# A two-layer decoder on one core: the order of projections, expert batches and rotations in layer 0, and six places in place of four in layer 1

## The reference

```python
# layer 0
qkv = x @ w_qkv.T                        # 32 query heads, 8 key/value heads, 64 wide
q, k = rope(rms(q) * wq), rope(rms(k) * wk)
a = softmax(q @ k.T / 8 + window_mask) @ v       # group "a"
x = layernorm(x + a @ w_out.T)           # norm x1; projection "out0"
q, k, v = x @ Wq, x @ Wk, x @ Wv         # 32 heads, 8 wide, rope
a  = softmax(q @ k.T + mask) @ v                 # "x", head groups 0..7, masked
a += tanh(gate) * softmax(q @ ak.T) @ av         # "x", groups 8..15, the adapter: keys and values of ctx
x = layernorm(x + a @ Wo)                # norm x2; projection "outx"
cw = top6(softmax(x @ gate_w.T))
for e in range(16):                      # experts, 176 wide
    y += cw[:, e] * (silu(x @ wg[e].T) * (x @ wu[e].T)) @ wd[e].T
x = layernorm(x + y)                     # norm x3
# layer 1: causal attention (16 heads), then attention of every row over all 1,024 rows of ctx
p = round(255 * softmax(q @ k.T)) / 255          # 16 heads x 8 tiles
x = layernorm(x + (p @ v) @ Wp + bp)
# then a gated feed-forward block with fp8-rounded weights
```

## Time and profile before

| | |
|---|---|
| median of 3 runs | 1586.13 us (1580.53 to 1587.86) |
| the profiled execution | 1585.61 us, of it 1583.70 us from the first to the last instruction |
| PE busy | 1339.4 us, 85% |
| DVE busy | 1078.7 us, 68% |
| ACT busy | 692.6 us, 44% |
| POOL busy | 112.0 us, 7% |
| granted TensorE clock, mean | 0.888 |
| layer 0 | to about 1107 us |
| causal attention of layer 1 | about 1107 to 1264 us |
| heads loop | about 1264 to 1480 us |
| feed-forward block | to the end |

### The profile page before, as it was taken

One profiled execution on the slowest core, in us unless ns is written; L12 is line 12 of the kernel. 1 busy time (PEld: TensorE's weight loads), 2 busy tenths in 40 slices (PEclk: granted clock), 3 DMA queues, 4 the chain that ended last, 5 costly groups with the idle time before them and its releaser, 6 DMA issues.

```text
span 1583.7 us, 24579 instructions
## 1 busy us (share of the span) xinstructions
PE 1339.4 (85%) x9229; PEld 881.4 (56%) x9234; DVE 1078.7 (68%) x2477; ACT 692.6 (44%) x1286; POOL 112.0 (7%) x95
## 2 busy tenths in 40 slices
PE   3868998998998999899899899999899678887576
PEld 1635765765765676576576567656777422222334
DVE  4458567556846756755684675564788789888577
ACT  1325434523632543452363254252444288787332
POOL 2020011002002001100200200000000000000001
PEclk9989999999999999999999999999999755555589
DMA  8200100100100010010010003100200089899300
GB/s 335 89 11 13 57 7 14 56 10 14 56 11 4 13 57 7 14 56 11 14 56 11 1 13 119 56 16 9 90 8 8 1 154 162 160 170 152 55 1 28
DMA packets 174517, 83.97 MB, mean 53 GB/s; under 512 B 137920, under 2 KB 170048, under 8 KB 173888
## 3 DMA queue, kind: packets, MB, share of 16 engines
q1 hardware_dynamic: 173248, 82.03, 21.1%
q10 hardware_dynamic: 1152, 0.36, 0.1%
HBM read 43.57 MB, written 5.24 MB: 31 GB/s over the span
## 4 chain that ended last, share of the span: by engine, by line
PE 47%; DVE 28%; issue 6%; ACT 6%; DMA 5%; POOL 1%; DVEq 0%; POOLq 0%; ACTq 0%
PE ps_p L1602 11%; PE ps_t L1618 10%; PE ps_s L1799 6%; DMA w_moe<-w_moe 5%; DVE w_moe L1491 4%; PE ps_o L1836 3%; DVE probs L1084 3%; PE ps_o L1679 3%; DVE row_max L1090 2%; PE ps_o L1799 2%; PE ps_p L1656 2%; PE ps_o L1683 2%; PE ps_t L1627 2%; PE ps_s L1656 1%; DVE probs L1075 1%
## 5 line engine op out<-in xcount | busy, mean ns | idle before, releaser
L1618 PE MATMUL ps_t<-ident,probs 128*128 128x128 f32 x1072 | 176.0, 286 | 27.6 <-ACT probs L820 11.3
L820 ACT ACTIVATE probs<-probs 128x512 f32<-128x512 f32 x192 | 120.9, 630 | 150.1 <-DVE probs L1084 150.1
L1618 PEld LDWEIGHTS ps_t<-ident,probs 128*128 128x128 f32 x1072 | 123.1, 144 | 79.6 <-issue 39.2
L790 ACT ACTIVATE probsT<-ps_t 128x512 f32<-128x512 f32 x232 | 136.4, 588 | 45.3 <-PE ps_t L1618 43.6
L1799 PE MATMUL ps_s<-w_moe,xbT 128*128 128x352 f32 x352 | 128.7, 492 | 0.0
L1985 PEld LDWEIGHTS ps_p<-vals,w_moe 128*128 128x128 f16 x1024 | 37.4, 106 | 149.6 <-DMA w_moe<-w_moe 140.5
L1602 PE MATMUL ps_p<-w_qkv,xinT 128*128 128x512 f32 (+1 forms) x240 | 115.0, 608 | 3.1 <-DVE ropes L1112 2.4
L743 POOL TENSOR_TENSOR rms<-mean_sq,neg_half 128x8 f32<-128x8 f32 x40 | 79.3, 1982 | 362.2 <-DVE mean_sq L1116 362.2
L1305 DVE SCALAR_TENSOR_TENSOR vals<-vals,ps_s 128x176 f32<-128x176 f32 x88 | 29.6, 336 | 106.6 <-ACT vals L871 104.8
L1799 PEld LDWEIGHTS ps_s<-w_moe,xbT 128*128 128x128 f32 x352 | 70.0, 207 | 36.8 <-issue 17.4
L1618 PE MATMUL ps_t<-ident,big 128*128 128x128 f32 x416 | 60.0, 281 | 32.8 <-DVE big L1131 32.5
(11 more groups left out here) (312 smaller groups left out, 2723.3 us busy)
## 6 DMA issues: line engine op xcount, KB each, us to landing
w_out<-in_wT_out SPq DMA_DIRECT2D x8, 2048.0 KB, 8.4
w_moe<-in_wT_gu SPq DMA_DIRECT2D x1, 5632.0 KB, 19.9
w_moe<-in_wT_down SPq DMA_DIRECT2D x1, 2816.0 KB, 27.0
w_qkv<-in_wT_qkv SPq DMA_DIRECT2D x1, 2048.0 KB, 9.5
keys<-keys2T SPq DMA_DIRECT2D x8, 256.0 KB, 2.0
keys2T<-keys SPq DMA_DIRECT2D x1, 2048.0 KB, 10.1
w_moe<-w_moe SPq DMA_TRANSPOSE x128, 3.3
w_qkv<-in_wT_qkv SPq DMA_DIRECT2D x2, 512.0 KB, 8.1
```

What stands on the lines that cost most here:

```text
L790: nc.scalar.activation(dst, src.bitcast(BF16) if dst.dtype == BF16 else src, ACT.Copy)\
L820: nc.scalar.activation(probs[:, at % 4, :], probs[:, at % 4, :], ACT.Exp).then_inc(L0.exped, 1)
L1618: ins = nc.tensor.transpose(dst[:, i * P:(i + 1) * P], src(i), ident_b[:] if bf else ident[:])
```

## The change

In layer 0 `MIXED` takes self-attention and masked groups in turn, so that all "a" groups lie in the first sixteen; the transposes "o0" go into the heads stage at steps 16, 17, 18 and 24, and blocks 0 to 11 of `out0` into steps 20 to 25, two to a step, into bank 1 of ps_o (it was a bank of ps_p). The fills of the last four groups and, for all but the first and the last tile, those of steps 0 and 1 are gone. The last down batch of tile b-1 runs behind the first scores of tile b, and norm x3 follows in steps 1 and 2. "k2", "ak" and "v2" stand in the projection stage. The rotations start at expert 3 and not at 9, one in two experts, and each scaling stands one expert behind its rotation. In layer 1 there are six buffers, and products lag five heads.

```diff
-MIXED = [("x", 0), ("a", 0), ("x", 1), ("x", 2), ("a", 1), ("x", 3), ("x", 4), ("a", 2), ("x", 5), ("a", 3), ("x", 6),
+MIXED = [("x", 0), ("a", 0), ("x", 1), ("a", 1), ("x", 2), ("a", 2), ("x", 3), ("a", 3), ("x", 4), ("x", 5), ("x", 6),
          ("x", 7)]
...
+O0_AT = {16: 0, 17: 1, 18: 2, 24: 3}
+OUT0_AT = {s: range(2 * s - 40, 2 * s - 38) for s in range(20, 26)}
...
-             9: [("r", 0), ("x", 3)], 10: [("r", 1), ("s", 0)], 11: [("r", 2), ("s", 1)], 12: [("x", 4)],
...
+             6: [("s", 1), ("x", 1)], 7: [("r", 2)], 8: [("s", 2), ("x", 2)], 9: [("r", 3)],
...
-TURNS = 4
-TURN_LAG = 6
+TURNS = 6
+SUM_LAG = 5
+TURN_LAG = 7
...
+            def o0_evac(b, j):
+                if mixed(b):
+
+                    act.wait_ge(L0.scores, G0.done(0, ("x", b, 2 * GX - 1 if j == 3 else GX - 1)))
+                evac(L0, ("o0", b + 1, j), flat(o0T[j]))
...
+                    if b >= 1 and s == 1:
+                        experts_norm_start(b - 1)
+                    if b >= 1 and s == 2:
+                        experts_norm_end(b - 1)
...
-                    normalise(("x1", n), ("out0", n), xin, xa)
+                    norm_start(("out0", n), xin)
+                    context_bias(n, "vt")
+                    norm_end(("x1", n), xa)
...
+            def out0(n, blocks):
+
+                if blocks[0] == 0:
+                    pe.wait_ge(out0_ready, n * KV0 + KV0)
+                    pe.wait_ge(ld_out0, n * 16 + 16)
+                for k in blocks:
+                    if k % 4 == 0:
+                        taken(L0, ("o0", n, k // 4))
+                    ins = nc.tensor.matmul(ps_o[:, 1, 0:D], o0T[k // 4][:, k % 4, :], w_out0[:, k, :], start=(k == 0),
+                                           stop=(k == 15))
+                if k == 15:
+                    ins.then_inc(out0_done, 1)
...
                     if s == 0 or s % 2 == 1 and s + 1 < len(groups):
                         pair_scores(groups[s + s % 2])
-                    if s < 2 and b >= 0:
+                    if s == 0 and b >= 1:
+                        down_batch(b - 1, len(HB) - 1)
+                    if s < 2 and b in (0, LAST):
+                        pe.wait_ge(L0.trans_taken, T0.at["p", *groups[0]])
                         dense(ps_t[:, 0, :], 3)
...
+                    if mixed(b) and s in O0_AT:
+                        o0_turn(b + 1, O0_AT[s])
+                    if mixed(b) and s in OUT0_AT:
+                        out0(b + 1, OUT0_AT[s])
...
                         transpose(L0, ("p", *group), lambda i: probs[:, at % 4, i * P:(i + 1) * P], GH,
-                                  fill=3 if b == LAST or s - 2 >= FILL_FROM and b >= 0 else 0,
+                                  fill=3 if b == LAST else 0,
...
-                    o0_turn(2)
-                    o0_turn(3)
-                    pe.wait_ge(ld_out0, n * 16 + 16)
-                    taken(L0, ("o0", n, 3))
-                    out0(range(0, 6))
+                    out0(n, range(12 if own else 0, 16))
+                    pe.wait_ge(ld_kv2, 16 * 2)
+                    project(L0, ("k2", n), ctxT, w_kv2, 0, D)
...
-                    out0(range(10, 16))
+                    pe.wait_ge(L0.proj_taken, P0.done(0, ("ck", n)))
+                    for i in range(2):
+                        transpose(L0, ("ak", n, i), lambda q: padded(ak_pad, 16 * i + 4 * q), 4)
+                    project(L0, ("v2", n), ctxT, w_kv2, D, D)
...
-            LAG = TURNS
-            for u in range(HEADS + LAG):
+            for u in range(HEADS + SUM_LAG):
```

More of the change, by code:

```diff
@@ L124, in transposes0 @@
                     keys.append(("h", b, *j))
-                elif what in ("ak", "c"):
-                    keys += [(what, n, 0), (what, n, 1)]
+                elif what == "c":
+                    keys += [("c", n, 0), ("c", n, 1)]
                 elif what == "x1":
@@ L879, in beside_experts @@
                             q0_evac(m, j[0])
-                        elif what == "ak":
-                            for i in range(2):
-                                evac(L0, ("ak", n, i), flat(akT[:, 4 * i:4 * i + 4, :]))
                         elif what == "x1":
@@ L1100, in rotate @@
                 dve.wait_ge(squared, t * 5 + c + 1)
+                if t and c < 2:
+                    dve.wait_ge(qkx_ready, t)
                 if c >= 2:
@@ L1290, in beside_experts @@
                     nc.vector.tensor_tensor(att[:], att[:], res[:], ALU.add).then_inc(heads_x, 1)
-                    normalise(("x2", b), ("outx", b), xa, xb)
+                if following:
+                    context_bias(n, "kf")
+                if own:
+                    norm_start(("outx", b), xa)
+                    norm_end(("x2", b), xb)
                 if following:
@@ L1749, in beside_experts @@
                 own, following = b >= 0, n < TILES
-                def o0_turn(j):
-                    pe.wait_ge(out0_ready, n * KV0 + 2 * j + 2)
-                    transpose(L0, ("o0", n, j), lambda i: big[:, (4 * j + i) * P:(4 * j + i + 1) * P], 4)
-                def out0(kk):
-                    project(L0, ("out0", n), bigT, w_out0, 0, D, kk)
                 pe.wait_ge(L0.shifted, G0.done(0, phase(b)[-1]))
+                if not own:
+                    for j in range(4):
+                        o0_turn(0, j)
                 if following:
-                    o0_turn(0)
-                    o0_turn(1)
                     pe.wait_ge(ld_w["att0"], 16 * 4)
@@ L1779, in beside_experts @@
                     transpose(L0, ("ox", b), lambda k: att[:, k * P:(k + 1) * P], KD)
-                if following:
-                    out0(range(6, 10))
-                if own:
                     taken(L0, ("ox", b))
@@ L1809, in beside_experts @@
                             q0_transposes(m, j[0])
-                        elif what == "ak":
-                            pe.wait_ge(L0.proj_taken, P0.done(0, ("ck", n)))
-                            for i in range(2):
-                                transpose(L0, ("ak", n, i), lambda q: padded(ak_pad, 16 * i + 4 * q), 4)
                         elif what == "x1":
```

134 lines of the change are left out of this document (81 added, 53 removed), and 4 rows, old and new, of the table AFTER.

## The result

| | before | after |
|---|---|---|
| median | 1586.12 us (1580.53 to 1587.86, 4 runs) | 1475.78 us (1474.80 to 1477.89, 4 runs) |
| span of the profiled execution | 1583.7 us | 1474.0 us |
| mean granted clock | 0.888 | 0.903 |

The ratio is 0.931 (95% interval 0.929 to 0.934): 110 us less, where 102 were forecast. A second set of runs of the changed kernel gave 1471.14 us (1469.91 to 1474.97).

The account below looks back on a forecast made before the run. PE was taken to bound layer 0's six periods, late DMA landings the layer 1 loop. Gains 6 x 11.9 + 5.8 + 1.5 + 23 = 101.7 us gave 1484 us, own range 1462 to 1512, 8-in-10 range 1445 to 1538.

Parts of the forecast that it names:

- Expert stage: Layer 0, experts part of each period: from 64.4 us to 51.0, with 48.7 us of PE work as lower bound.
- the chain of DVE and POOL: In the expert stage, rotations, powers and scalings cost DVE 7.0 us per two experts, against PE's 6.1.
- Heads stage: Layer 0, heads part of each period: 52.4 us of work plus 2.5 idle, 54.9 us in place of 54.1.
- Projection stage: Layer 0, projection part of each period: from 14.5 us to 10.7, with 8.4 us of work.
- The clock: Layer 0 periods: 3.4 us of clock loss left in each, half of today's, making 120.0 us a period.
- Outside the six periods: Tile 6's projection stage and last heads stage's start gain 3.8 + 2.0; earlier rotations ahead of tile 0 gain 1.5.
- The heads loop: Layer 1: one more step of lag hides late landings, step from 1.63 us to 1.45, gaining 23 us.
- The lower end: Layer 1 loop at DVE's 1.37 us for every step, a gain of 33 us.
- The upper end: Layer 1 loop bound by DMA engines, 93% busy, at 1.52 us a step, a gain of 14 us.
- full gain: Rival, chance 0.17: layer 0 clock stays up and layer 1 loop runs at 1.37; gain 132, 1454 us.
- Half gain: Rival, chance 0.18: scalings wait longer than 1.4 us, experts queue, loop DMA-bound; gain 52, 1534 us.
- Slower: the clock: Rival, chance 0.05: unfilled heads stages fall to clock 0.50 for good, 1830 us; half at half speed, about 1660.

Follow-up runs that it names:

- the lag runs: Changed kernel with four buffers, products four heads behind: 1490.4 us; six buffers, four heads behind: 1493.7 us; eight buffers, seven heads behind: 1470.0 us.
- eight buffers: Changed kernel with eight buffers instead of six and products seven heads behind instead of five: 1470.0 us, 0.927 of the kernel before.
- lag of four: Changed kernel with its six buffers kept, but products four heads behind instead of five: 1493.7 us, 0.943 of the kernel before.
- first tile: Changed kernel with fills in the stage ahead of tile 0 and its norm x1 ended before the bias of v2: 1473.9 us, 0.930 of before.

## Why the prediction was right, step by step

The forecast, 1484, was 8 us above the result, inside its own range. Part of that closeness is luck: the six periods gave 20.6 us more than forecast, and the rest of the program 8.6 us and the heads loop 4.0 us less, so that errors of 33 us in all left 8. Against its steps:

- **Expert stage**: 51.0 forecast, 49.57 measured; PE's work 47.97 (48.7). DVE waits 1.1 us for a power and not 1.4, and PE waits for DVE nowhere in this stage: the chain of DVE and POOL, which the forecast took for the bound, keeps ahead of PE.
- **Heads stage**: 54.9 forecast, 55.82 measured, PE's idle time 2.6 us (2.5), busy 95% (95). The work was 0.8 more than priced; half of that is the starting value, 50.4 - 3.4 = 47.0, where the stage at clock 1.00 shows 47.4.
- **Projection stage**: 10.7 forecast, 10.88 measured. No stage shows a wait of `out0` for its weights. The three stages sum to 116.3, against 116.6, because the expert stage's -1.4 and the heads stage's +0.9 nearly cancel.
- **The clock**: 3.4 us a period left, none found in five of six (116.3 us; the first took 118.0, its expert stage at 0.97). This step was mis-sized, and it is the largest error: the six periods gave 92.0 us and not 71.4. Today's loss was sized too high as well: 64.4 x 0.05 is 3.2 and not 3.4, and of the six heads stages before only four lost anything, 3.0 us each. What the runs show is that a long wait brought back brings losses back right behind it (2.1 and 2.2 us in the expert stage, 1.8 in the heads stage), and that in the new order, with no wait over 0.8 us, the clock holds without fills. They do not show a rule: some waits of 2 us cost nothing, and some stages lose clock behind waits of 0.8 us and less.
- **Outside the six periods**: +7.3 forecast, and 1.3 us lost. The step that failed is the accounting. Tile 6's projection stage (3.8) lies inside the periods and was counted already; the one outside is tile 0's. And tile 0's heads stage also takes the blocks and "o0", which was left out: it took 57.1 us and not 51.9, at clock 0.94. By norm x1 of tile 1, 3.7 us were lost ahead of the periods. Of these 1.8 stand ahead of the first scores of all (47.6 us and not 45.8) and 1.3 from there to norm x1 of tile 0, neither of which was forecast. Between norm x1 of tiles 0 and 1 the rotations brought 1.4 (forecast 1.5), the heads stage lost 5.2 and the projection stage gave back 3.2. Behind norm x1 of tile 7, up to the heads loop, 2.4 were won.
- **The heads loop**: 23 forecast, 19.0 measured; the step 1.48 and not 1.45. The mechanism is shown by the lag runs. The lower end was set too low: "DVE's 1.37 at every step" leaves out DVE's 7 x 1.08 = 7.6 us at the ends of tiles, which is why no lag can go under 182.8. The upper end, DMA engines at 1.52, is refuted by the steps of 1.38. PE's waits for DMA fell to 103.6, not below 80. The total was a poor sign: with eight buffers these waits are down to 6.6 us, and the loop is only 5.4 us shorter.

92.0 - 1.3 + 19.0 = 109.7, the difference between the spans.

By parts undone one at a time, against 1471 to 1476 us: rotations 53 to 58, down batch 24 to 29, lag and buffers 15 to 19, `out0` 14 to 19, fills put back 15 to 20. They overlap through the clock and need not add up. The moves of "k2", "ak", "v2" and the order of `MIXED` were not tried alone.

The rivals: full gain (1454) failed outside the periods and in the loop's 7.6 us; inside the periods it was right. Half gain needed scalings that wait over 1.4 us; the longest was 1.1 in that stage. "Slower: the clock" was not what happened. A milder form of it is what the old kernel shows without its fills, 0.85 to 0.94 in the heads stages and not 0.50 for good.

## What to carry to other kernels

Price an idle stretch of TensorE twice, as its length and as what the clock gives away behind it: here the clock added 4.0 us to 5.2 of waits for rotations, and 1.6 to 4.2 to one wait of 1.8. Look for the loss right behind each long wait, in short stretches of the clock, and not in a stage's mean. Before you fill a wait, read which instruction it stands ahead of: eight fill products one transpose too early were 1.9 us of work and filled nothing. Real work is the best filler: in the order without long waits, fills cost 2.6 us a period and bought nothing. In a ring of buffers it is the distance between issue and use that hides a latency, and buffers only make room for it; before you name a loop's bound, look for the work that one engine does only every sixteenth step.

## What was not expected of the hardware

- The same instructions with the same waits do not always run at the same clock. The expert stage of the changed kernel took 49.57 us at clock 1.00, or 51.26 at 0.97, with the same three waits of PE (0.6, 0.6 and 0.3 us). With no change in those tiles, the last of the six periods took 120.5 or 120.6 us and not 116.3 in three profiles (eight buffers, lag of four, first tile); each was the longest of its four executions.
- Waits of 2.1 and 1.9 us in an expert stage at clock 1.00 cost nothing in two of six periods of one kernel, and waits of the same length cost some 3 us of clock in the kernel before, in all six.
- DMA transposes land a median 3.3 us after issue with four and with six buffers and 3.4 with eight, and 5.0 to 5.4 us at worst in six profiles, at 160 to 179 GB/s. The landing with eight in flight, 5.1 at worst, is no later than with four.
